# Pre-convolution in two rounds of 108 rows with four tap loads a step, and row statistics turned and sent earlier

## The reference

```python
x1 = _conv(x[:, :dc], w_pc, 'SAME')             # 12 of 48 channels, 3x3
x = jnp.concatenate([x1, x[:, dc:]], axis=1)
x = _conv(x, w_in, 'VALID')                     # 1x1, 48 -> 254
xp = x.reshape(B, C, H // P, P, W // P, P).transpose(0, 1, 2, 4, 3, 5)
xp = jnp.fft.irfft2(jnp.fft.rfft2(xp) * fft_w, s=(P, P))    # 8x8 patches
a, b = jnp.split(x, 2, axis=1)
x = jax.nn.gelu(a, approximate=False) * b
return _conv(x, w_out, 'VALID')                 # 1x1, 127 -> 48
...
x = x + _L0_conv_ref(_ln_c(x), w_pc, w_in, fft_w, w_out)
t = _to_tokens(x)
t = t + _L0_ffn_ref(_ln_t(t), W1, b1, W2, b2)   # 48 -> 192 -> 48, operands quantized to fp8
```

## Time and profile before

| | us | share of the span |
|---|---|---|
| median of 3 runs | 702.02 | |
| the profiled execution | 702.13 | |
| its span, first to last instruction | 700.3 | |
| PE busy | 664.4 | 95% |
| PEld busy | 522.9 | 75% |
| DVE busy | 596.9 | 85% |
| ACT busy | 536.6 | 77% |
| POOL busy | 460.9 | 66% |

### The profile page before, as it was taken

The page is one execution under the profiler, slowest core; times in us unless marked ns, Lnnn a source line. Parts: engine busy times, 40 slices in busy tenths (PEclk is TensorE's granted clock), DMA queues, the critical chain, the costliest instruction groups (busy, mean ns, idle before and its releaser), DMA issues.

```text
span 700.3 us, 19259 instructions
## 1 busy us (share of the span) xinstructions
PE 664.4 (95%) x6713; PEld 522.9 (75%) x6713; DVE 596.9 (85%) x1151; ACT 536.6 (77%) x1080; POOL 460.9 (66%) x355
## 2 busy tenths in 40 slices
PE   1689999999999999999999999999999999999984
PEld 1577778877777788777877887778778877787751
DVE  5537888889898889898999888988988899877877
ACT  3144479888888898888888988888889888877784
POOL 2555656778667767786776677867676777653353
PEclk9999999999999999999999999999999999999995
DMA  3443333333434343344344432343444324331102
GB/s 83 87 104 89 86 73 102 99 79 90 106 91 109 94 105 94 81 92 103 93 109 94 107 102 74 89 106 91 101 102 105 100 59 109 78 85 46 47 22 69
DMA packets 47959, 62.23 MB, mean 89 GB/s; under 512 B 20607, under 2 KB 36439, under 8 KB 47863
## 3 DMA queue, kind: packets, MB, share of 16 engines
q1 hardware_dynamic: 45015, 60.52, 34.9%
q10 hardware_dynamic: 2848, 0.48, 0.4%
HBM read 44.62 MB, written 16.35 MB: 87 GB/s over the span
## 4 chain that ended last, share of the span: by engine, by line
PE 87%; DVE 6%; SPq 2%; issue 2%; POOL 1%; ACT 1%; DMA 0%; DVEq 0%; ACTq 0%; POOLq 0%
PE inva L483 16%; PE invb L490 16%; PE mixp L470 13%; PE misc L734 8%; PE misc L499 7%; PE misc L554 4%; PE misc L520 4%; PE misc L598 4%; PE misc L470 3%; PE misc L719 3%; PE misc L529 2%; PE mixp L567 2%; PE misc L588 2%; PE mixp L574 2%; DVE gmix L1144 1%
## 5 line engine op out<-in xcount | busy, mean ns | idle before, releaser
L483 PEld LDWEIGHTS inva<-inv,gmix 128*127 128x127 f32 x1024 | 126.2, 191 | 16.5 <-DVE gmix L1144 11.5
L483 PE MATMUL inva<-inv,gmix 128*127 128x128 f32 x1024 | 137.9, 277 | 0.6 <-DVE gmix L1144 0.6
L490 PE MATMUL invb<-inv,gmix 128*127 128x128 f32 x1024 | 134.7, 274 | 0.2
L1144 DVE TENSOR_TENSOR gmix<-mixp,freq_w 128x508 f32<-128x508 f32 x192 | 122.7, 681 | 14.0 <-PE mixp L470 13.5
L1452 POOL TENSOR_TENSOR st<-st,neg_half 128x16 f32<-128x16 f32 x32 | 92.8, 2899 | 60.6 <-DVE st L1366 60.6
L490 PEld LDWEIGHTS invb<-inv,gmix 128*127 128x127 f32 x1024 | 123.7, 191 | 1.4 <-DVE hbuf L1155 0.6
L816 ACT ACTIVATE hid<-misc 128x512 f16<-128x512 f32 x180 | 98.0, 601 | 17.6 <-PE misc L554 17.6
L1155 DVE TENSOR_TENSOR hbuf<-gact,invb 127x512 f32<-127x512 f32 x128 | 87.5, 684 | 24.3 <-ACT gact L808 18.7
L1483 POOL TENSOR_TENSOR st<-st,neg_half 128x16 f32<-128x16 f32 x31 | 95.4, 3077 | 16.4 <-DVE st L1223 16.4
L825 ACT ACTIVATE hid<-hid 128x512 fp8e5<-128x512 f16 x174 | 93.2, 618 | 0.0
L808 ACT ACTIVATE gact<-inva 127x512 f32<-127x512 f32 x128 | 76.9, 601 | 20.6 <-PE inva L483 20.0
(11 more groups left out here) (178 smaller groups left out, 1369.2 us busy)
## 6 DMA issues: line engine op xcount, KB each, us to landing
xin<-in_x_dram SPq DMA_DIRECT2D x64, 192.0 KB, 3.3
xres<-in_x_dram SPq DMA_DIRECT2D x64, 192.0 KB, 4.2
out_dram<-ob SPq DMA_DIRECT2D x60, 192.0 KB, 2.7
taps<-cz_scratch SPq DMA_DIRECT2D x32, 292.5 KB
crm<-rm_scratch SPq DMA_DIRECT2D x64, 96.0 KB
cz_scratch<-cz SPq DMA_DIRECT2D x64, 48.8 KB
cx<-in_x_dram SPq DMA_DIRECT2D x32, 96.0 KB
rm_scratch<-rm_t SPq DMA_DIRECT2D x120, 4.0 KB
```

The lines of the kernel that those rows point to most:

```text
L483: mm = pe.matmul(inva[0:HID, q * PX:(q + 1) * PX], gmix[:, s % 2, q, 0:HID], inv[:], start=True, stop=True, skip_group_check=True)
L490: mm = pe.matmul(invb[0:HID, q * PX:(q + 1) * PX], gmix[:, s % 2, q, HID:HID2], inv[:], start=True, stop=True, skip_group_check=True)
L1144: dve.tensor_tensor(gmix[:, s % 2, 2 * q:2 * q + 2, 0:HID2], pair[q][:, 0:2 * HID2].rearrange("p (e c) -> p e c", e=2), freq_w[:], ALU.mul ...
```

## The change

The taps now take 108 partitions: 72 (24 planes by 3 vertical offsets) at one horizontal offset, and below them 36 (12 planes by 3) at a second one. Two such arrangements stand beside each other in the tile. The first holds offset 0 for both parts and offset 1 for the high part, the second offset 2 for both and offset 1 for the low part. Four DMAs fill them, two of 72 and two of 36 partitions. `stream` has two rounds of four matmuls, 8 in place of 12. The weights are laid out to match, still with 6 small loads at the start.

`rows` on PE moves from between the halves of `inverse(1)` to behind `turn_tokens`, ahead of `turn_rest`, for every step from 3 to 31; there it writes `mixp[0]` instead of `bank[3]`. `mix` 2, which writes `mixp[0]`, now waits for ACT's copy of it. On ACT, `rows` moves from behind the first accumulator to ahead of `tokens`. On SP, `rows_out` stands ahead of the wait for POOL's output and of the output stores; `rows_in` stays behind them.

```diff
-KP = 2 * 3 * CC
+KP = 3 * 3 * CC
+TAPS = SROW * PW - 2
...
-                    for part in range(2):
-                        for dx in range(3):
-                            sp.dma_start(raw_pc[part * 3 * CC:(part + 1) * 3 * CC, dx, :],
+                    for turn in range(2):
+                        for block, dx in ((0, 2 * turn), (1, 2 * turn), (2, 1)):
+                            sp.dma_start(raw_pc[block * 3 * CC:(block + 1) * 3 * CC, turn, :],
                                          w_pc[:, :, :, dx].rearrange("o i dy -> (i dy) o")).then_inc(const_in, 16)
...
-                    src = bass.AP(cz_d.tensor, rows16(c) * PW, [[PLANE, 2 * CC], [PW, 3], [1, SROW * PW]])
-                    sp.dma_start(taps[:], src).then_inc(col_in, 16)
+                    for turn in range(2):
+                        both = bass.AP(cz_d.tensor, rows16(c) * PW + 2 * turn, [[PLANE, 2 * CC], [PW, 3], [1, TAPS]])
+                        sp.dma_start(taps[0:6 * CC, turn, 0:TAPS], both).then_inc(col_in, 16)
+                        one = bass.AP(cz_d.tensor, rows16(c) * PW + turn * CC * PLANE + 1,
+                                      [[PLANE, CC], [PW, 3], [1, TAPS]])
+                        sp.dma_start(taps[6 * CC:KP, turn, 0:TAPS], one).then_inc(col_in, 16)
+                if live(t, 0) and a > 2:
+                    rows_out(t)
                 if live(t, 6):
...
                 if live(t, 0) and not early:
-                    rows_out(t)
+                    if a == 2:
+                        rows_out(t)
                     rows_in(t)
...
-                for dx in range(3):
+                for turn in range(2):
+                    rows = taps[:, turn].rearrange("p (r w) -> p r w", w=PW)
                     for g in range(4):
...
-                        mm = pe.matmul(bank[3][32 * g:32 * g + 32, :], wpc[:, dx, :], src,
-                                       start=(dx == 0), stop=(dx == 2), skip_group_check=True)
+                        src = rows[:, :, 2 * TW * g:2 * TW * (g + 1)].rearrange("p r (i w) -> p i r w", w=TW)
+                        mm = pe.matmul(bank[3][32 * g:32 * g + 32, :], wpc[:, turn, :], src,
+                                       start=(turn == 0), stop=(turn == 1), skip_group_check=True)
...
                 pe.wait_ge(rmT_ready, upto(a))
-                pe.wait_ge(tsq_ready, upto(2 * m + 2))
-                pe.transpose(bank[3][0:32, 0:128], rm[:].rearrange("p a j i -> p (a j i)"), eye[:])\
+                if a < 3:
+                    pe.wait_ge(tsq_ready, upto(2 * m + 2))
+                dst = bank[3]
+                if a > 2:
+                    pe.wait_ge(gmix_ready, upto(8 * n + 2))
+                    pe.wait_ge(y16_ready, upto(2 * at(t, 6) + 2))
+                    dst = mixp[0]
+                pe.transpose(dst[0:32, 0:128], rm[:].rearrange("p a j i -> p (a j i)"), eye[:])\
...
                 if live(t, 5):
                     turn_tokens(t)
+                if live(t, 0) and live(t, 3):
+                    rows(t, 0)
                 if live(t, 4):
                     turn_rest(t)
                 if live(t, 3):
                     pe.wait_ge(y16_ready, upto(2 * l + 2))
+                    pe.wait_ge(rmT_ready, upto(a + 1, STEPS))
                     mix(t, 2)
...
-                    inverse(t, 3, 1, (lambda: rows(t, 0)) if turn else None)
+                    inverse(t, 3, 1)
...
                     gelu(t, 3, 0)
+                if live(t, 0) and not filling:
+                    rows(t, 0)
                 if live(t, 5):
                     tokens(t)
...
-                if live(t, 0) and not filling:
-                    rows(t, 0)
```

More of the change, by code:

```diff
@@ L97, in metaformer_kernel @@
         raw_w2 = sb("raw_w2", [CH, FF])
-        raw_pc = sb("raw_pc", [KP, 3, CC])
+        raw_pc = sb("raw_pc", [KP, 2, CC])
         raw_b = sb("raw_b", [128, 3])
@@ L106, in metaformer_kernel @@
         wout = sb("wout", [HID, HALF])
-        pc32 = sb("pc32", [KP, 3, CC])
-        wpc = sb("wpc", [KP, 3, 32], F16)
+        pc32 = sb("pc32", [KP, 2, CC])
+        wpc = sb("wpc", [KP, 2, 32], F16)
         l1 = sb("l1", [128, 3, 128], F8)
@@ L131, in metaformer_kernel @@
         cz16 = sb("cz16", [CC * CG, 2, 2, 2, PW], F16)
-        taps = sb("taps", [KP, SROW * PW], F16)
+        taps = sb("taps", [KP, 2, SROW * PW], F16)
         convs = sb("convs", [128, 4, PX])
@@ L513, in stream @@
                     pe.wait_ge(rmT_ready, upto(a + 1))
-                pe.wait_ge(col_in, upto(16 * (c + 1)))
-                rows = taps[:].rearrange("p (r w) -> p r w", w=PW)
-                for dx in range(3):
+                pe.wait_ge(col_in, upto(64 * (c + 1)))
+                for turn in range(2):
+                    rows = taps[:, turn].rearrange("p (r w) -> p r w", w=PW)
                     for g in range(4):
-                        w0 = 2 * TW * g + dx
-                        src = rows[:, :, w0:w0 + 2 * TW].rearrange("p r (i w) -> p i r w", w=TW)
-                        mm = pe.matmul(bank[3][32 * g:32 * g + 32, :], wpc[:, dx, :], src,
-                                       start=(dx == 0), stop=(dx == 2), skip_group_check=True)
+                        src = rows[:, :, 2 * TW * g:2 * TW * (g + 1)].rearrange("p r (i w) -> p i r w", w=TW)
+                        mm = pe.matmul(bank[3][32 * g:32 * g + 32, :], wpc[:, turn, :], src,
+                                       start=(turn == 0), stop=(turn == 1), skip_group_check=True)
                 mm.then_inc(stream_done, 1)
@@ L833, in rows @@
                     act.wait_ge(rm_out, upto(64 * (a - 1)))
-                act.activation((rm_t1 if second else rm_t)[:], bank[3][0:32, 0:128], ACT.Copy).then_inc(rmT_ready, 1)
+                act.activation((rm_t1 if second else rm_t)[:], (mixp[0] if a > 2 else bank[3])[0:32, 0:128], ACT.Copy).then_inc(rmT_ready, 1)
             def rows_out(t, behind):
```

## The result

The changed kernel takes 707.51 us (median; 707.16 to 709.40), the kernel before in the same session 701.94 (701.40 to 702.33). The ratio is 1.0077, with a 95% interval of 1.0062 to 1.0092: slower by 0.8%. The forecast was 704.2 with a range up to 707.2; the direction is right, the size is short by 3.3 us, and the time lies just outside the range.

The account below looks back on a forecast made before the run. PE was taken to bound the kernel. Full steps +0.8, step 3 +1.9, step 4 +0.8, step 5 +0.1, step 2 +0.5, end -0.5, disturbances -1.5 sum to +2.1 us on 702.13: 704.2, range 700.0 to 707.2.

Parts of the forecast that it names:

- The usual step: Steps 6 to 31: later third `hidden`, moved turn and shorter stream nearly cancel; +0.03 us a step, +0.8 for 26.
- The wait: PE's third `hidden` matmul waits for ACT's delayed `tsq` in nearly every step; it starts 0.42 us later.
- Rival B: Full steps: third `hidden` doesn't wait, so the shorter stream is pure gain, 26 x (-0.28), 696 us; chance 0.12.
- the bound: Full steps, lower bound: -0.25 us a step if the third `hidden`'s wait doesn't appear, -6.5 in all.
- The disturbances and the end: Earlier POOL `cz` removes all disturbances, -1.5 us; steps 32 and 33 stream and turn no rows, -0.5 us.
- Steps 4 and 5: Fill: step 4's turn waits for DVE's `rm`, +0.8 us; step 5 has slack under the third `hidden`, +0.1.
- Step 2, the tap loads: Fill: the last of four tap loads lands at 38.6 to 39.3 and the stream waits; +0.5 us.
- Step 3: Fill: `mix` 2 waits for the early turn of `rm` and ACT's copy; +1.9 us with the shorter stream.
- rival E: The clock falls in step 3's gap, so `mix` 2 and `inverse(1)` slow: +2.8 us, 707.0; chance 0.08.

Follow-up runs that it names:

- The two queues: The changed kernel, with step 2's two tap loads of the second round issued by ACT while SP issues the first two: 706.93 us, ratio 1.0070.
- the stream alone: The kernel before with only the stream changed (two rounds of 108 rows, four tap loads), row statistics at their old place: 718.32 us, ratio 1.0203.
- the clock held: The changed kernel with more idle `keep_busy` matmuls in the holes of steps 2 and 3, every wait staying: 706.44 us, ratio 1.0038.
- the order alone: The changed kernel with the stream of before (three rounds of 72 rows, one tap load), only the order changed: 711.93 us, ratio 1.0132.

## Why the prediction was right in its direction and wrong in its size

Measured values are differences of the two profiled executions, 7.3 us in all; by the medians the loss is 5.6, so part of what follows is larger than in the median execution.

- **The usual step: right.** Forecast +0.03 a step, measured -0.04 (19.95 to 19.91). The wait appeared where it was put, in 30 steps. The third `hidden` came 0.32 us later within its step, forecast 0.42: ACT's pause and copy cost `tsq` 0.41 in place of 0.49. For 26 steps this is 1.8 us better than the sum had it. That this wait is real and set by ACT, the copy between the halves of `tokens` shows: it gave back 0.22 a step. (Rival B's price was worked out with -0.28 a step, the bound with -0.25; with the bound's value B would be 697, not 696.)
- **The disturbances and the end: right.** POOL's `cz` starts early (after up to 0.3 us of idle time in most steps, 1.0 in the worst), the steps of 20.36 are gone (498.04 - 25 x 19.91 = 0.3 us are left of 1.5), and without SP's part the long DVE operations are back, and the end gained 0.6, forecast 0.5.
- **Steps 4 and 5: right,** +0.7 and +0.1.
- **Step 2, the tap loads: the term that was mis-sized.** Forecast +0.5, measured +3.5. I let each load land 3.3 us after its issue, by the median of another, single load, as if only the last issue counted. But four loads share one set of engines: three times the bytes of before, 5.3 us of packets, 7.4 us from the first issue to the stream. The two queues show that the issues don't set it, and one load in steps 2 and 3 gives back 2.8 us of step 2 (17.97 to 15.14). The prediction's own words had the answer for full steps, since "issued 6 us and more ahead" is less than 7.4 (in the trace before it is 5.4 to 8.1). It is only the moved rows, which start SP's chain 2.3 us earlier, that make it enough; the stream alone, and the whole change without SP's part, end 2.0% and 2.6% above before. The forecast had SP's part as a gain against disturbances, not as the condition for the loads.
- **Step 3: the wait right, the clock wrong.** With the clock held step 3 takes 18.69, which is +1.9 over before, and +1.9 was the forecast; the turn stands 11.23 us into the step (56.16), where the forecast had it (52.27 of a step from 41.04). The other 3.8 us are rival E, to which I gave 0.08 with the argument that "the one matmul in the gap speaks against it". It doesn't keep the clock: with one short matmul at 56.89 between 54.08 and 57.62 the clock fell, at 56.96, and with the order alone it fell at 53.17, behind the turn at 52.53. The rule of the Trainium skill ("TensorE: Matmul & The Clock Gate", Part 1) that was cited there, the clock falls when PE has been idle for a while, is borne out by these holes; that of 3.15 us in the run with two queues drew no fall. Its price was not right either: forecast 2.8. Where step 3's hole alone drew a fall, which lasted 3.4 us, it cost 1.6 (two queues, 20.25 against 18.69) and at most 1.8 (order alone, 20.49, with a round more). The changed kernel's 3.8 are more, since the hole of step 2, which the forecast didn't have, drew a stretch at 1.2 GHz that reaches 2.0 us into step 3, and the second stretch lasted 6.8 us there.

So of the 5.2 us between forecast (+2.1) and profile (+7.3), step 2 makes +3.0 and the clock in step 3 +3.8, and the steady part gives back 1.8; small terms are the rest. Two steps failed: the landing of the tap loads in step 2, mis-sized at +0.5, and the clock behind the holes, put at nothing. Shown by experiment are the round's 0.26, the wait of the third `hidden`, the cover that the loads need, and the parts of step 3. The idle matmuls gave back 3.0 us of span and 2.7 by the ratios, not the whole 3.8. Open is why the tap transfer runs below the rate that other stretches of the trace reach.

## What to carry to other kernels

A load that grows from one transfer to four was timed here by its transfer as a whole and from its first issue (7.4 us, 5.3 of them packets), not by a single load's landing; ask for every step how many microseconds of cover there are, in the fill first, where there are fewest. Work moved forward on a dense engine is cheap or dear by half a microsecond of place: ahead of `tokens` the copy waited for its producer and delayed the chain behind, between its halves it cost the step nothing. And a wait in the fill is to be priced with the clock behind it: in step 3 the wait itself cost 1.9 us and the lower clock another 3.8, which idle matmuls in the holes took away.

## What the hardware showed unexpectedly

The lower clock can come late: PE began to work again at 41.53 and the clock fell at 43.3, in the middle of dense work, for 3.4 us; at the second hole it fell as PE began again (56.96) and lasted 6.8 us. In the run with the stream alone it fell inside a wait, at 546.06 of one that ended at 546.90. And it does not come each time: a hole of 2.77 us in step 2 drew it, one of 3.15 us at the same place, with two queues, did not. So a wait of about the same length costs a varying time from one kernel to the next: step 3, with the same wait for `rm`, took 22.5 us in the changed kernel and 20.3 with two queues. The other finding is the tap transfer: 0.91 MB in 5.3 us, 172 GB/s, whether its issues start over 2.4 us on one queue or over 0.9 us on two.
